# Layer 1's maxima over the whole array, from a copy of one head's queries that is zero outside the head, and a new order of the mixed phase

## The chip, the cores and the metric

The kernel runs on one core of a Trainium2 chip. The metric is device time in microseconds of one launch, which works through all sixteen graphs of the input; lower is better. "Before" is the kernel as it stands, "the change" the edited one.

## The reference, cut to what matters

Sixteen graphs of 512 nodes with 256 channels pass through two attention layers. Layer 0 has one head with a 0/1 mask, layer 1 eight heads of 32 channels with a weight per edge:

```python
# layer 0
scores = jnp.einsum('bod,bid->boi', q, k) / denom
scores = jnp.where(mask, -1e+18, scores)
attn = jax.nn.softmax(scores, axis=2)
ctx = jnp.einsum('boi,bie->boe', attn, node_fts) @ Wc
x = layer_norm(node_fts + ctx)
# layer 1: H = 8 heads, DK = 32
logits = jnp.einsum('bhqd,bhkd->bhqk', q, k) / np.sqrt(DK)
logits = logits + jnp.log(jnp.clip(adj, ADJ_MIN, None))[:, None, :, :]
attn = jax.nn.softmax(logits, axis=-1)
out = jnp.einsum('bhqk,bhkd->bhqd', attn, v)
out = out @ Wo.T + bo
x = layer_norm(x + out)
```

The softmax of layer 1 is computed as exp(logit - row maximum) times the clipped edge weight, divided by its sum. The row maxima are taken from a product of rounded queries and keys alone; they only shift the exponent.

## The kernel before

Every engine follows one list of stages, written out as a table. A phase of the mixed kind works on three graphs at once: the tail of graph t (project, stats1, norm1, output), the back of graph i (layer 1: scores1, masks, values1, denominators1, maxima of the second group of heads) and the front of graph j (layer 0, then q1, k1, v and the maxima of the first group). The list `SCHEDULE` sets the order of the mixed phase, `FIRST` that of the opening one and `LAST` that of the one that has no front any more. Each engine takes from the list, in that order, the stages that it has a part in, so one list fixes five queues. There are 15 mixed phases (one of them without a tail), between an opening phase for graph 0 and the closing ones.

The eight heads are two groups g of four heads h; 128 channels of a group lie on 128 partitions, head h on partitions 32h to 32h+31. The names that the rows show are:

- `max1` (g, n): TensorE (L709) multiplies 128 queries of one head by its 512 keys, with 32 rows of the array, into one of four shared `misc` banks of PSUM; VectorE (L1026) reduces the 512 columns to a negated maximum in `mx`. There are 32 a phase. n runs over query tile t and head h, with h fastest, so that neighbours in the list lie in different row groups of the array.
- `mrow1` (L714, L1032): the maxima of a group, turned into a row; after it the row goes by DMA into the stack `QS`.
- `scores1` (L730, ScalarE's exponential L868): keys x queries from the stacks `QS` and `KS` of 97 rows (three 32-row parts and the row of maxima), into two banks `scores`. `mask` (L1168 on GpSimd, L1011 on VectorE for the pairs that the list names) multiplies the result `PR` by the edge weights `CLIP`. A quad is four such products; `PR` has three buffers, quad modulo 3.
- `values1`, `denominators1` (L753): four 32-column products each, side by side in four column groups of the array, eight instructions a quad.
- `q0`, `q1`, `k1` (L609), `u` (L619), `v` (L631), `max0` (L661, L663), `scores0` (L674, L678, L679), `context0` (L687), `transpose` (L696), `project` (L775): products over the whole array. Their banks are drained by ScalarE or VectorE. Products of full 4-byte operands (L687, L696, L714, L753) are executed in two passes, and the profile counts both: four products of L753 in the program are eight in a row of it.
- `high_output` (L886, ScalarE) and `low_output` (L1083, VectorE) split the normalised output into `OTH` and `OTL`, which `project` multiplies.

The `misc` banks are handed out in the order of the list, modulo four; a fill waits until the use before it in the same bank is drained. TensorE takes its instructions in order, so that a product that waits holds everything behind it. The operand of a maximum is cut out like this:

```python
t, h = divmod(n, PER_GROUP)
part = slice(DK * h, DK * (h + 1))
pe.matmul(bank[:], Q1H[part, g, P * t:P * (t + 1)], K1H[part, g, :],
          start=True, stop=True).then_inc(misc_filled, 1)
```

## Time and profile before

| | us |
|---|---|
| median of the 3 runs | 1225.13 |
| the runs | 1222.51, 1225.13, 1558.84 |
| the profiled execution | 1222.59 |
| its span | 1220.8 |
| opening phase (0 to 78.58) | 78.58 |
| 15 mixed phases (78.58 to 1146.20) | 1067.62 |
| one of them (504.04 to 575.38) | 71.34 |
| closing phases (1146.20 to 1220.80) | 74.60 |

Shares of the span in which an engine is busy: TensorE (PE) 94%, its weight loads (PEld) 56%, VectorE (DVE) 77%, ScalarE (ACT) 43%, GpSimd (POOL) 60%. The 1.8 us between the profiled execution's time and its span lie around the span. A phase is counted from the first instruction of `mrow1` of group 0 (L714) to the next one; all times "at 5xx" are those of the phase that begins at 504.04. A duration of a product that the profile shows is from its start to its modelled end; products overlap in the pipeline, so what one costs TensorE is the distance from its start to the start of the next.

### The profile page before, as it was taken

How to read it: one execution, taken by the hardware profiler on the slowest of the kernel's cores; microseconds unless marked ns; L12 is line 12 of the kernel's file. 1: busy time of each engine (PE TensorE's matmuls, PEld its weight loads, DVE VectorE, ACT ScalarE, POOL GpSimd, SP SyncE). 2: the span in 40 equal slices, each digit the busy share in tenths (PEclk: the TensorE clock that was granted, in tenths of full speed). 3: DMA queues.
4: the chain of work that ended last, by engine and by line, in shares of the span. 5: the costliest groups of instructions: out<-in, count | busy, mean ns of one | idle time of the engine just before them, and what ended most of it. 6: DMA issues, size and time to landing. Idle time of an engine off the chain costs nothing.

```text
span 1220.8 us, 21304 instructions
## 1 busy us (share of the span) xinstructions
PE 1146.4 (94%) x6474; PEld 684.3 (56%) x6474; DVE 934.1 (77%) x1733; ACT 524.4 (43%) x1021; POOL 738.0 (60%) x353
## 2 busy tenths in 40 slices
PE   7789999999999999999999999999999999999883
PEld 6555564656556465564656556464655646565431
DVE  4465877969687796968779696877969688796874
ACT  3233444445344444534444453444445344444431
POOL 1026486584848658484865848487584848757462
PEclk9889999999999999999999999999999999999887
DMA  3051331405132140513314051331405133140310
GB/s 130 1 139 35 107 85 45 129 17 143 46 108 82 43 129 17 142 48 107 82 41 131 17 140 50 106 84 41 132 17 139 50 103 86 39 133 17 90 31 17
DMA packets 69652, 94.67 MB, mean 78 GB/s; under 512 B 14081, under 2 KB 32769, under 8 KB 69634
## 3 DMA queue, kind: packets, MB, share of 16 engines
q1 hardware_dynamic: 69634, 94.44, 27.5%
q8 instruction: 10, 0.16, 0.1%
q14 instruction: 8, 0.07, 0.0%
HBM read 35.40 MB, written 8.39 MB: 36 GB/s over the span
## 4 chain that ended last, share of the span: by engine, by line
PE 40%; DVE 23%; POOL 18%; issue 12%; ACT 5%; DVEq 0%; POOLq 0%; DMA 0%; ACTq 0%; SPq 0%
PE misc L609 11%; DVE mx L1026 8%; POOL PR L1168 8%; PE scores L730 6%; PE misc L631 4%; PE misc L619 3%; POOL z L1182 3%; POOL res L1151 3%; PE misc L661 2%; PE misc L709 2%; DVE PR L1011 2%; PE values L753 2%; PE values L775 2%; DVE K1L L990 2%; DVE sums_w L1073 2%
## 5 line engine op out<-in xcount | busy, mean ns | idle before, releaser
L1168 POOL TENSOR_TENSOR PR<-PR,CLIP 128x1024 f32<-128x1024 f32 x217 | 543.3, 2528 | 372.8 <-ACT PR L868 372.8
L1026 DVE TENSOR_REDUCE mx<-misc 128x1 f32<-128x512 f32 x512 | 322.4, 680 | 92.7 <-PE misc L709 92.4
L868 ACT ACTIVATE PR<-scores 128x512 f32<-128x512 f32 x512 | 279.2, 601 | 226.6 <-PE scores L730 217.8
L730 PE MATMUL scores<-QS,KS 97*128 97x512 f32 x512 | 196.4, 460 | 9.0 <-issue 3.5
L753 PE MATMUL values<-PR,V 128*32 128x512 f32 x1024 | 133.2, 603 | 14.5 <-DVE PR L1011 14.4
L753 PE MATMUL denominators<-PR,ones 128*32 128x512 f32 x1024 | 133.9, 605 | 0.8 <-DVE z L1092 0.3
L730 PEld LDWEIGHTS scores<-QS,KS 97*128 97x128 f32 x512 | 89.6, 193 | 68.3 <-ACT PR L868 36.3
L709 PE MATMUL misc<-K1H,Q1H 32*128 32x512 f32 x512 | 119.4, 500 | 6.7 <-DVE K1L L990 1.6
L687 PE MATMUL misc<-U,P 128*128 128x257 f32 x512 | 121.8, 386 | 0.0
L1073 DVE RECIPROCAL sums_w<-sums_w 128x128 f32<-128x128 f32 x128 | 114.0, 924 | 7.0 <-ACT sums_w L881 4.2
L709 PEld LDWEIGHTS misc<-K1H,Q1H 32*128 32x128 f32 x512 | 48.0, 183 | 119.2 <-DVE mx L1026 63.6
L687 PEld LDWEIGHTS misc<-U,P 128*128 128x128 f32 x512 | 94.4, 189 | 20.0 <-issue 3.8
L856 ACT ACTIVATE P<-misc 128x512 f32<-128x512 f32 x64 | 38.3, 598 | 96.4 <-PE misc L679 96.4
L753 PEld LDWEIGHTS values<-PR,V 128*32 128x32 f32 x1024 | 25.1, 109 | 68.9 <-issue 44.4
L1011 DVE TENSOR_TENSOR PR<-PR,CLIP 128x1024 f32<-128x1024 f32 x39 | 59.6, 1535 | 1.9 <-ACT PR L868 1.8
L674 PE MATMUL misc<-Q0H,XTH 128*128 128x512 f32 x128 | 58.9, 460 | 0.0
L834 ACT COPY V<-misc 128x512 f32<-128x512 f32 x32 | 18.8, 586 | 89.7 <-PE misc L631 89.7
L1182 POOL TENSOR_TENSOR z<-z,spread 128x1024 f32<-128x1024 f32 x16 | 38.2, 2390 | 28.8 <-DVE z L1108 28.8
L990 DVE SCALAR_TENSOR_TENSOR Q1L<-misc,cols,Q1H 128x512 fp32r<-128x512 f32 x32 | 24.0, 751 | 39.6 <-ACT Q1H L829 39.6
L753 PEld LDWEIGHTS denominators<-PR,ones 128*32 128x32 f32 x1024 | 22.4, 108 | 52.7 <-issue 46.2
L674 PE MATMUL misc<-Q0L,XTH 128*128 128x512 f32 x128 | 50.9, 398 | 0.0
L674 PE MATMUL misc<-Q0H,XTL 128*128 128x512 f32 x128 | 50.8, 397 | 0.0
(160 smaller groups left out, 1896.3 us busy)
## 6 DMA issues: line engine op xcount, KB each, us to landing
ADJ<-adj_t SPq DMA_DIRECT2D x16, 1024.0 KB, 6.0
QS<-Q1H SPq DMA_DIRECT2D x256, 64.0 KB, 2.0
KS<-K1H SPq DMA_DIRECT2D x256, 64.0 KB, 2.0
P<-x_t SPq DMA_DIRECT2D x16, 512.0 KB, 3.8
X<-x SPq DMA_DIRECT2D x16, 512.0 KB, 3.7
QS<-Q1L SPq DMA_DIRECT2D x128, 64.0 KB, 2.0
KS<-K1L SPq DMA_DIRECT2D x128, 64.0 KB, 2.0
out<-z SPq DMA_DIRECT2D x16, 512.0 KB, 2.9
```

Source lines behind the costliest of these rows:

```text
L609: mm = pe.matmul(bank[:], w[:, k, P * c:P * (c + 1)], s[:, k, :], start=(n == 0), stop=(n == len(terms) - 1))
L674: pe.matmul(bank[:], kk[:, c, rows_k], qq[:, c, :], start=(n == 0), stop=False)
L687: mm = pe.matmul(bank[:, 0:D + 1], P0[:, k, P * t:P * (t + 1)], U[:, k, 0:D + 1], start=(k == 0), stop=(k == T - 1))
L709: pe.matmul(bank[:], Q1H[part, g, P * t:P * (t + 1)], K1H[part, g, :], start=True, stop=True).then_inc(misc_filled, 1)
L730: pe.matmul(ST[n][:], KS[:, h, P * k:P * (k + 1)], QS[:, h, :], start=True, stop=True).then_inc(scores_filled, 1)
L753: mm = pe.matmul(bank[DK * h:DK * (h + 1), :], w, PR[quad % WEIGHT_BUFFERS][:, h, :], start=(k == 0), stop=(k == T - 1))
L868: act.activation(PR[quad % WEIGHT_BUFFERS][:, h, :], ST[n][:], ACT.Exp, scale=SCALE1).then_inc(exp_done, 1)
L1011: dve.tensor_tensor(w, w, clipped, ALU.mult).then_inc(masked_dve, 1)
L1026: dve.tensor_reduce(mx1[:, g, h, t:t + 1], misc_bank(ph, "max1", g, n)[:], AX.X, ALU.max, negate=True).then_inc(misc_drained["dve"], 1)
L1073: dve.reciprocal(sums_w[:, q], sums_w[:, q]).then_inc(back_step, 1)
L1168: pool.tensor_tensor(w, w, clipped, ALU.mult).then_inc(masked_pool, 1)
L1182: pool.tensor_tensor(z[:], z[:], all_rows(S_G1), ALU.mult).then_inc(pool_step1, 1)
```

## The change

The queries of one head are copied by ScalarE into `QZ[:, h, :]`, an array that was set to zero once, so that 96 of its 128 rows are zero. A maximum then is a product of all 128 rows, `QZ[:, h]` by `K1H[:, g]`. There are four such copies a group, eight a phase, as a new stage `alone` (g, h). n now runs over head and query tile with the tile fastest. The list of the mixed phase is written anew; `FIRST` and `LAST` get the copies put in and are otherwise the same. VectorE clears `QZ` once at the start.

```diff
 SCHEDULE = [
-    ("reciprocal", 1, 0), ("skip_back",), ("split", 0), ("split", 1), ("max1", 1, 0), ("reciprocal", 1, 1),
...
+    ("reciprocal", 1, 0), ("alone", 1, 0), ("split", 0), ("split", 1), ("alone", 1, 1), ("max1", 1, 0),
...
+        QZ = sb("QZ", [P, PER_GROUP, N], F32R)
...
+        def alone(ph, g, h):
+
+            return HEADS * (ph.i if g else ph.j) + PER_GROUP * g + h + 1
...
                 bank = fill(ph, "max1", g, n)
-                t, h = divmod(n, PER_GROUP)
-                part = slice(DK * h, DK * (h + 1))
-                pe.matmul(bank[:], Q1H[part, g, P * t:P * (t + 1)], K1H[part, g, :],
+                h, t = divmod(n, T)
+                if t == 0:
+                    pe.wait_ge(head_alone, alone(ph, g, h))
+                pe.matmul(bank[:], QZ[:, h, P * t:P * (t + 1)], K1H[:, g, :],
                           start=True, stop=True).then_inc(misc_filled, 1)
...
+            def put_alone(ph, g, h):
+                part = slice(DK * h, DK * (h + 1))
+                if g == 0:
+                    act.wait_ge(hi_written, ph.j * (C * len(SPLIT)) + nth_split(ph, "q1", 0))
+                    if ph.back:
+                        wait_filled(act, ph, "max1", 1, T * h + T - 1)
+                else:
+                    act.wait_ge(misc_drained["dve"], misc.count_before(ph, "max1", 0, T * h + T - 1))
+                act.copy(QZ[part, h, :], Q1H[part, g, :]).then_inc(head_alone, 1)
...
+            dve.memset(QZ[:].bitcast(F32), 0.0).then_inc(consts_set, 1)
...
             def max1(ph, g, n):
-                t, h = divmod(n, PER_GROUP)
+                h, t = divmod(n, T)
```

The new list moves work on every engine. TensorE at the end of a mixed phase, from `k1` of channel half 1 to `mrow1` (maxima are L709 before and L722 after, the products of 32 columns L753 and L766, `v` L631 and L643). Before:

```order
L609 MATMUL misc<-XNL,Wk_high 128x512 x2
L709 MATMUL misc<-K1H,Q1H 128x512
L753 MATMUL denominators<-PR,ones 32x512 x4
L709 MATMUL misc<-K1H,Q1H 128x512 x2
L753 MATMUL values<-PR,V 32x512 x4
L709 MATMUL misc<-K1H,Q1H 128x512 x3
L631 MATMUL misc<-Wv_high,XNH 128x256 x2
...
L709 MATMUL misc<-K1H,Q1H 128x512 x2
L631 MATMUL misc<-Wv_high,XNH 128x256 x2
...
L714 MATMUL misc<-ident,mx 16x128
```

and with the change:

```order
L621 MATMUL misc<-XNL,Wk_high 128x512 x2
L722 MATMUL misc<-K1H,QZ 128x512 x3
L766 MATMUL denominators<-PR,ones 32x512 x4
L766 MATMUL values<-PR,V 32x512 x8
L722 MATMUL misc<-K1H,QZ 128x512 x4
L643 MATMUL misc<-Wv_high,XNH 128x256 x2
...
L722 MATMUL misc<-K1H,QZ 128x512 x5
L643 MATMUL misc<-Wv_high,XNH 128x256 x2
...
L727 MATMUL misc<-ident,mx 16x128
```

Twelve maxima instead of eight now stand behind `k1`, and the products of 32 columns, which stood between maxima in two places, have become one group.

VectorE in the same stretch, from the low part of `q1` to the end of the phase (`K1L`, `Q1L` are L990 and L1015, the maxima L1026 and L1051, the clipping L999 and L1024, `OTL` L1083 and L1108). Before:

```order
L990 SCALAR_TENSOR_TENSOR Q1L<-misc,cols,Q1H 128x512
L990 SCALAR_TENSOR_TENSOR K1L<-misc,cols,K1H 128x512
L1079 TENSOR_TENSOR sums_v<-sums_v,sums_w 128x512
L1026 TENSOR_REDUCE mx<-misc 128x1 x3
L990 SCALAR_TENSOR_TENSOR Q1L<-misc,cols,Q1H 128x512
L1026 TENSOR_REDUCE mx<-misc 128x1 x3
L999 TENSOR_SCALAR CLIP<-ADJ 128x2048
L1026 TENSOR_REDUCE mx<-misc 128x1 x2
L990 SCALAR_TENSOR_TENSOR K1L<-misc,cols,K1H 128x512
L1026 TENSOR_REDUCE mx<-misc 128x1 x8
L1083 TENSOR_TENSOR OTL<-sums_v,OTH 128x512
L1032 CAST nm_0<-misc 16x128
```

and with the change:

```order
L1015 SCALAR_TENSOR_TENSOR Q1L<-misc,cols,Q1H 128x512
L1015 SCALAR_TENSOR_TENSOR K1L<-misc,cols,K1H 128x512
L1015 SCALAR_TENSOR_TENSOR Q1L<-misc,cols,Q1H 128x512
L1104 TENSOR_TENSOR sums_v<-sums_v,sums_w 128x512
L1051 TENSOR_REDUCE mx<-misc 128x1 x4
L1024 TENSOR_SCALAR CLIP<-ADJ 128x2048
L1015 SCALAR_TENSOR_TENSOR K1L<-misc,cols,K1H 128x512
L1051 TENSOR_REDUCE mx<-misc 128x1 x3
L1108 TENSOR_TENSOR OTL<-sums_v,OTH 128x512
L1051 TENSOR_REDUCE mx<-misc 128x1 x9
L1057 CAST nm_0<-misc 16x128
```

All sixteen maxima of the group now come after the second `Q1L`; three stood ahead of it.

ScalarE in the loop, where `OTH` (L886 and L909) is written for the projection (L868 and L891 are exponentials, L840 and L863 drain `u`; ISA and REGISTER_ALU rows are waits and their counters). Before:

```order
L840 COPY U<-misc 128x258
L885 ISA
L886 CAST OTH<-sums_v 128x512
L867 REGISTER_ALU
L868 ACTIVATE PR<-scores 128x512
```

and with the change:

```order
L863 COPY U<-misc 128x258
L890 REGISTER_ALU
L891 ACTIVATE PR<-scores 128x512
L890 REGISTER_ALU
L891 ACTIVATE PR<-scores 128x512
L908 ISA
L909 CAST OTH<-sums_v 128x512
```

Two exponentials have moved ahead of `OTH`.

## Rows read from the trace of the kernel before

**Rows 1.** Windows: span, busy us (xcount) of PE, PEld, DVE, ACT, POOL, granted clock, DMA.

```profile
504.04:575.38 71.34, 69.38 (x401) 41.39 (x401) 56.86 (x107) 32.29 (x63) 46.96 (x22) 1.00 0.28 81
78.58:1146.20 1067.62, 1038.89 (x5976) 618.19 (x5977) 843.04 (x1569) 483.24 (x943) 697.23 (x326) 1.00 0.28 79
1146.20:1220.80 74.60, 45.58 (x229) 20.42 (x228) 49.63 (x76) 22.25 (x41) 35.30 (x17) 0.74 0.14 38
```

**Rows 2.** Timeline, TensorE, maxima and their neighbours: start us, us, engine line op.

```profile
517.59 0.40 PE L663 MATMUL misc<-masked_bf,ABSENT 128*128 128x128 bf16 x4
517.91 0.50 PE L709 MATMUL misc<-K1H,Q1H 32*128 32x512 f32 x2
518.34 0.72 PE L730 MATMUL scores<-QS,KS 97*128 97x512 f32 x2
...
521.85 0.51 PE L709 MATMUL misc<-K1H,Q1H 32*128 32x512 f32 x4
522.28 1.92 PE L753 MATMUL values<-PR,V 128*32 128x512 f32 x16
524.14 0.50 PE L709 MATMUL misc<-K1H,Q1H 32*128 32x512 f32 x2
524.57 1.06 PE L753 MATMUL denominators<-PR,ones 128*32 128x512 f32 x8
525.57 0.50 PE L674 MATMUL misc<-Q0H,XTH 128*128 128x512 f32 x1
525.91 0.39 PE L674 MATMUL misc<-Q0H,XTL 128*128 128x512 f32 x1
526.14 0.39 PE L674 MATMUL misc<-Q0L,XTH 128*128 128x512 f32 x1
```

**Rows 3.** Timeline, TensorE, the start of the phase.

```profile
504.04 0.39 PE L714 MATMUL misc<-ident,mx 128*16 128x128 f32 x2
504.58 0.69 PE L709 MATMUL misc<-K1H,Q1H 32*128 32x512 f32 x2
505.79 1.01 PE L609 MATMUL misc<-XTH,A_high 128*128 128x512 f32 x2 [0.52 <-ACT XTH L822]
```

**Rows 4.** Timeline, TensorE, transposes and the wait for a mask.

```profile
550.61 1.08 PE L696 MATMUL misc<-ident,xn 128*128 128x128 f32 x4
551.45 0.77 PE L730 MATMUL scores<-QS,KS 97*128 97x512 f32 x2
...
555.26 1.06 PE L753 MATMUL values<-PR,V 128*32 128x512 f32 x8 [0.95 <-DVE PR L1011]
```

**Rows 5.** Timeline, TensorE, three maxima near the end, then v.

```profile
570.77 0.84 PE L709 MATMUL misc<-K1H,Q1H 32*128 32x512 f32 x3
571.71 0.50 PE L631 MATMUL misc<-Wv_high,XNH 128*128 128x256 f32 x2
```

**Rows 6.** Timeline, ScalarE, VectorE and TensorE around the projection.

```profile
516.37 0.62 ACT L886 CAST OTH<-sums_v 128x512 fp32r<-128x512 f32 x1
...
517.41 1.60 DVE L1083 TENSOR_TENSOR OTL<-sums_v,OTH 128x512 fp32r<-128x512 f32 x1
...
519.38 0.40 PE L775 MATMUL values<-Wo_high,OTL 128*128 128x256 f32 x2
```

**Rows 7.** Timeline, VectorE, clipping, low part of k1, six maxima.

```profile
566.79 1.22 DVE L999 TENSOR_SCALAR CLIP<-ADJ 128x2048 f32<-128x2048 f32 x1
...
569.12 0.74 DVE L990 SCALAR_TENSOR_TENSOR K1L<-misc,cols,K1H 128x512 fp32r<-128x512 f32 x1
569.78 3.67 DVE L1026 TENSOR_REDUCE mx<-misc 128x1 f32<-128x512 f32 x6
```

**Rows 8.** Timeline, ScalarE, two copies from SBUF to SBUF.

```profile
576.45 1.15 ACT L822 CAST XTH<-P 128x512 fp32r<-128x512 f32 x2
```

**Rows 9.** Groups by line, VectorE, a memset of the start.

```profile
L919 DVE MEMSET PR<- 128x256 f32 x1 | 0.3, 272 | 0.0
```

**Rows 10.** The page, costliest groups: the masks on GpSimd.

```profile
L1168 POOL TENSOR_TENSOR PR<-PR,CLIP 128x1024 f32<-128x1024 f32 x217 | 543.3, 2528 | 372.8 <-ACT PR L868 372.8
```

More of the change, by code:

```diff
@@ L150, in is_back @@
 def is_back(stage):
-    return stage[0] in BACK or stage[:2] in (("max1", 1), ("mrow1", 1))
+    return stage[0] in BACK or stage[:2] in (("alone", 1), ("max1", 1), ("mrow1", 1))
 def is_tail(stage):
@@ L365, in two_layer_graph_attention @@
         hi_written = sem("hi_written")
+        head_alone = sem("head_alone")
         bias_built = sem("bias_built")
@@ L404, in two_layer_graph_attention @@
         FOLDED_LOADS, FIRST_LOADS, REST_LOADS = 2, 1 + 1, 4 + 1
-        CONSTS = 9
+        CONSTS = 10
         block = ctx.enter_context(nc.Block())
@@ L421, in graph_of, with nth_split @@
             return ph.t if g == GROUPS - 1 else ph.i
+        def alone(ph, g, h):
+            return HEADS * (ph.i if g else ph.j) + PER_GROUP * g + h + 1
+        def nth_split(ph, *stage):
+            return [s for s in ORDERS[ph.kind] if s[0] in SPLIT].index(stage) + 1
         def mask_operands(quad, pair):
@@ L899, in _ @@
                 "k1": lambda ph, c: hi(ph, "k1", c, K1H, BK1),
+                "alone": put_alone,
                 "v": lambda ph, n: rows_out(ph, "v", n, V),
```

9 lines of the change are left out of this document (5 added, 4 removed), and 73 rows, old and new, of tables (FIRST, LAST, SCHEDULE).

## The prediction

> **What bounds the kernel now.** I read the windows first. The 15 mixed phases take 1067.62 of the span's 1220.8 us, 71.2 each, and the one that I follow takes 71.34, with TensorE busy for 69.38 of it at the full clock, VectorE for 56.86, GpSimd for 46.96 and ScalarE for 32.29 [rows 1]. So TensorE's queue sets the phase; what matters is what an instruction costs there and where the queue stands still. The timeline of TensorE tells both, by distances from start to start.
>
> The price of a whole-array product of 512 columns is 0.23 us (525.91 to 526.14) [rows 2]. Maxima go otherwise: two of them hold TensorE for 0.43 us (517.91 to 518.34) and four for the same 0.43 (521.85 to 522.28) [rows 2]. Row groups work side by side, but a run costs 0.43 whether it holds one or four. On top, each change between the whole array and a divided one costs some 0.10: the first product after a divided stretch takes 0.34 and the next 0.23 [rows 2]; on the way in, four short products take 0.32 up to a maximum (517.59 to 517.91) [rows 2], where my price for them, 0.21, makes 0.11.
>
> The queue stands still in few places. At the phase's start, mrow1 and two maxima take 1.75 us (504.04 to 505.79), and q0 then waits for XTH from ScalarE [rows 3]; 0.43 for the maxima and 0.32 for mrow1 leave 1.0 lost. Transposes waiting for xn take 0.84 instead of 0.44 (550.61 to 551.45), a sum waits 0.95 for a mask of VectorE [rows 4], and three maxima near the end take 0.94 instead of 0.43, since their banks are still to be drained [rows 5]. With some 1.0 in small pieces, mostly around score products, I count 3.9 us of waiting and 67.4 of work a phase.
>
> **The price of the maxima.** The new list has the same 32 a phase. Before they stand in 13 runs: 13 x 0.43 = 5.6 us. After, 32 x 0.23 = 7.4. That is +1.8. The clock is at its upper level of 2.4 GHz (granted 1.00) in this stretch and TensorE's activity rises if anything, so I leave the price at that level.
>
> A rule of the Trainium skill speaks against the change: "TensorE: Matmul & The Clock Gate", section "Why this matters for your kernels", has small-K products in distinct row groups run concurrently, 3.07 times faster for four, and a single K=32 product as long as a K=128 one. The trace here gives 4 x 0.23 / 0.43 = 2.1 for a run of four and worse than that page for a single one. By the page a run would cost 4 x 0.23 / 3.07 = 0.30, the runs before 3.9 us in all, and the change +3.5 where the rows give +1.8: 25 us more over 15 phases. The rows are of this kernel and decide.
>
> **The changes of mode.** Going through the list of before, TensorE's divided stretches (maxima and the 32-column sums, where they adjoin each other) number 12, so 24 changes. After, maxima no longer divide the array and the sums stand in 6 groups, 12 changes. 12 x 0.10 = -1.2. The sums' own price stays: sixteen in a row cost 1.86 (522.28 to 524.14), eight cost 1.00 (524.57 to 525.57) [rows 2], so each switch of bank costs about 0.14, and both lists have 14 stretches of one bank.
>
> Work on the array therefore changes by 1.8 - 1.2 = **+0.6 us a phase** before any wait is looked at. The new order has to win it back from the 3.9 us of waiting.
>
> **The waits.** I follow the new list with the prices above, in the time of the phase shown, and ask where it stands against before.
> - Start. One maximum instead of two stands ahead of q0, so that is cheaper, but q0 waits for XTH either way. On ScalarE a copy of a head stands ahead of XTH where a copy of the sums stood before; a copy from SBUF to SBUF costs 0.58 (1.15 for two) [rows 8]. No gain until q0. ABSENT is now built ahead of both low parts of q0, and max0 needs the second one: 0.1 lost.
> - Projection. Before, OTH is written at 516.37, OTL by VectorE from 517.41 for 1.60 us, and TensorE asks for OTL at 519.38 [rows 6], 0.4 after it is there. Now two exponentials precede OTH, which puts it at about 517.7, and a max1 and a max0 precede OTL, which then ends near 519.9. TensorE asks for it near 519.3. It waits 0.6, and everything behind it: three maxima, a score pair, scores0. GpSimd gets the last mask of quad 2 about 1 us later, and with it the norm of the tail.
> - Middle, up to context0. Eleven maxima cost 2.5 instead of four runs of 0.43, and two groups of sums stand alone: +0.9. I have TensorE 1.7 us behind by context0.
> - Transposes. GpSimd has lost one mask (3,0 goes to VectorE) and reaches the norm of the front a little earlier, while TensorE comes later: the 0.4 and the 0.95 of [rows 4] go. What is late next is ScalarE: scores1 of quad 6 wait for exponentials, 0.7 again in front of the sums. 1.1 behind at q1.
> - End. q1, k1, q1 and two score pairs stand together: 3 x 1.4 + 2 x 0.5 us, so that the second Q1H is ready near 563.1. From then on VectorE has Q1L, normalise, sixteen maxima, clip, K1L and OTL without a gap: maxima at 0.61 (3.67 for six), clip 1.15, K1L 0.66, the starts being 566.79, 569.12 and 569.78 [rows 7]; I take 0.68 for the other three. 16 x 0.61 + 1.15 + 4 x 0.68 = 13.6, end at 576.7, and mrow1 follows there instead of at 575.38: +1.4. Before, three of the maxima were done ahead of the second Q1L. v must wait for their banks in turn, so TensorE has nothing to overtake with.
> - Next start. The sums are copied before v now, and the start's loss of 1.0 shrinks by 0.3 since TensorE arrives later than ScalarE's work allows.
>
> So the walk gives +1.1 a phase, the bare price of the work with waits as before +0.6. I take +0.9: 15 x 0.9 = **+13.5**. The eight copies are 8 x 0.58 = 4.6 us on ScalarE, busy 32.29 of 71.34; they hide there behind waits for TensorE, except the one ahead of XTH. If that cover is gone they cost 0.58 each where an exponential waits for one: 15 x 0.58 = 9 for each such place.
>
> **Opening and closing.** The memset of QZ is 128x2048; 128x256 takes 0.272 [rows 9], so at most eight times that, 2.2, and nothing at the least if it lies beside the first loads. I take 0.5. In the opening, four copies stand ahead of K1H and VectorE sets the pace of maxima: +0.5. The closing phase of 74.60 has the clock at 0.74 on average, so partly at 1.2 GHz [rows 1]; its sixteen maxima stand in 8 runs: 8 x 0.43 = 3.4 becomes 16 x 0.23 = 3.7, and up to 16 changes of mode at 0.10 go. That is -1.3, or -2.6 if all of it ran at half the clock, but the chain there goes through exponentials and masks as well, and three copies stand among those (1.7 if each is on the path). I take -0.5, bounds -3 and +2.
>
> **Sum.** 13.5 + 0.5 + 0.5 - 0.5 = +14. The profiled execution's 1222.6 (span 1220.8 plus 1.8 around it) becomes 1236.6; the median of the runs stands 2.5 above it, so **1239 us**, +1.1%.
>
> **Rivals.**
> 1. The new order takes out half of the waiting (for it: it does remove the waits of [rows 4], and a single whole-array product can be put anywhere without a change of mode; against: I found new waits at OTL and at the end). 3.9 falls to 1.9, a phase changes by 0.6 - 2.0 = -1.4, 15 phases by -21: 1225 - 21 = 1204.
> 2. Slower, through GpSimd. It runs the chain norm of the tail, two steps of z, two of res, three masks, norm of the front, and then xn for the transposes. A mask costs 2.5 [rows 10] and the other steps about as much; seven of them are 17.5 us. With the last mask of quad 2 late by 1.1 and norm1 behind four maxima, z begins near 530.5 and xn is there near 549.8, while TensorE asks at 551.5. The slack is 1.7. If z begins later than 532.2, the chain decides and every further microsecond is added to the phase; 1.5 beyond it, with the rest of my walk, makes +2.4 a phase, +36: 1261.
> 3. The change costs what the work costs and the waits cancel: +0.6 x 15 = +9, 1234. A whole-array maximum that took 0.27, as one behind a short product may, would add 32 x 0.04 = 1.3 a phase: +19 on top of the forecast, 1257.
> 4. The maxima do not bound anything, because VectorE's reduce (0.61 against 0.23) paces them anyway: then only the order counts, and the time stays within 5 us of 1225.
>
> **Chances.** Forecast and the first half of rival 3 together 0.50 (1228 to 1248); rival 1 0.20, of which 0.08 beyond 2%; rival 2 and the dear product 0.18; rival 4 0.12. The range that leaves out 1 in 10 on either side is 1204 to 1260; the unknown costs of opening and closing (-3 to +4) lie within it. Two per cent, 24.5 us, is about what a measurement can tell from no change: faster 0.09, same 0.68, slower 0.23.
>
> **What would show it.** In the profile after: the distance between whole-array maxima in a run, 0.23 each; mixed phases of about 72.2 us between the mrow1 of group 0; no wait of a sum for VectorE's mask near 555; a wait of the projection for OTL of about 0.6; VectorE without a gap from the second Q1L to the end of the phase. The prediction is wrong if a phase is under 70.5 (waits gone that I kept) or over 73.5 (GpSimd's chain, or a price of 0.27), or if the clock in the closing phase moves by more than the copies cost.

## The result and the profile after

The change takes 1247.15 us (median of 1236.40, 1244.99, 1249.32 and 1251.35) against 1229.33 for the kernel before in the same comparison. The ratio of its runs to those of before is 1.0158, with a 95% interval of 1.0111 to 1.0205: slower by some 1.6%, 8 us above the 1239 of the prediction and inside its range. The 1229.33 counts a slow run of before, of 1558.84 us, which the ratio leaves out; its other three runs have a median of 1225.13. The profiled execution took 1236.4 us, the shortest of the four, with a span of 1234.6; that is 0.2 us from the forecast for it, 1236.6. That agreement is luck, as the parts show.

Windows of the kernel with the change: the phase that begins at 507.62, the 15 mixed phases, the closing (columns as in [rows 1]):

```profile
507.62:579.07 71.45, 69.97 (x399) 45.03 (x401) 57.36 (x106) 37.09 (x72) 47.86 (x22) 1.00 0.29 80
76.82:1154.26 1077.44, 1048.18 (x5947) 672.42 (x5977) 861.01 (x1569) 555.94 (x1065) 709.64 (x326) 1.00 0.28 79
1154.26:1234.60 80.34, 48.66 (x228) 23.23 (x228) 48.83 (x75) 24.37 (x44) 34.29 (x17) 0.74 0.13 36
```

Against [rows 1] the mixed phases are 9.8 us longer, the closing 5.7, the opening 1.8 shorter: together the 13.8 by which the spans differ. The mean of 0.65 a phase hides two kinds. Cut at the mrow1 of group 0, ten mixed phases take 71.4 to 71.7 us, nearly as before (71.3 to 71.4), four take 73.35, and the very first, without a tail, takes 69.5 instead of 68.75. The phase of the first row is a short one, only 0.1 above its counterpart.

What bounds it is told by the page's chain that ended last. Before, the chain went through GpSimd for 18% and VectorE for 23%; now:

```profile
PE 77%; DVE 12%; issue 4%; ACT 4%; POOL 0%; DVEq 0%; ACTq 0%; DMA 0%; POOLq 0%; SPq 0%
```

So TensorE's queue is the bound in the main, with VectorE for an eighth of the time. The timeline of TensorE answers [rows 2] (price of a product), [rows 3] (start) and [rows 4] (transposes, then sums):

```profile
507.62 0.39 PE L727 MATMUL misc<-ident,mx 128*16 128x128 f32 x2 [0.19 <-DVE mx L1051]
508.75 0.49 PE L722 MATMUL misc<-K1H,QZ 128*128 128x512 f32 x1 [0.74 <-ACT QZ L853]
509.26 1.02 PE L621 MATMUL misc<-XTH,A_high 128*128 128x512 f32 x2
...
525.52 0.85 PE L722 MATMUL misc<-K1H,QZ 128*128 128x512 f32 x3
526.21 0.63 PE L743 MATMUL scores<-QS,KS 97*128 97x512 f32 x2
...
532.75 0.50 PE L722 MATMUL misc<-K1H,QZ 128*128 128x512 f32 x1
533.09 0.39 PE L686 MATMUL misc<-Q0H,XTH 128*128 128x512 f32 x1
...
555.20 0.60 PE L708 MATMUL misc<-ident,xn 128*128 128x128 f32 x4
555.84 0.99 PE L743 MATMUL scores<-QS,KS 97*128 97x512 f32 x2
556.76 1.07 PE L766 MATMUL denominators<-PR,ones 128*32 128x512 f32 x8
```

Three maxima take 0.69 (525.52 to 526.21), 0.23 each; one behind a divided stretch takes 0.34 (532.75 to 533.09), the 0.10 of a change of mode again. That is the price where the banks are free. Where VectorE still drains them it is higher, as in the last two runs of the phase:

```profile
572.59 1.20 PE L722 MATMUL misc<-K1H,QZ 128*128 128x512 f32 x4
573.88 0.51 PE L643 MATMUL misc<-Wv_high,XNH 128*128 128x256 f32 x2
...
575.42 1.68 PE L722 MATMUL misc<-K1H,QZ 128*128 128x512 f32 x5
577.20 0.51 PE L643 MATMUL misc<-Wv_high,XNH 128*128 128x256 f32 x2
```

Four take 1.29 and five 1.78. From mrow1 to q0 it is 1.64 instead of 1.75, and the wait is for the first copy now, 0.74, where it was 0.52 for XTH. Transposes and sums no longer wait for xn or for a mask.

The waits of TensorE over all mixed phases say the same in four rows, "us in total, times, longest":

```profile
PE misc L722 <- ACT QZ L853: 11.3, 15, 0.8
PE values L788 <- DVE OTL L1108: 6.6, 4, 1.7
PE misc L727 <- DVE mx L1051: 2.5, 14, 0.2
PE misc L727 <- issue: 2.4, 15, 0.2
```

Before these were 14.4 for VectorE's mask and 7.1 for XTH. The OTL row has four waits: they are the four long phases.

A short and a long phase at the projection ([rows 6] before). VectorE and TensorE in the phase from 507.62:

```profile
521.51 0.69 DVE L1040 TENSOR_REDUCE bounds<-misc 128x1 f32<-128x512 f32 x1
522.12 0.68 DVE L1108 TENSOR_TENSOR OTL<-sums_v,OTH 128x512 fp32r<-128x512 f32 x1
...
523.14 0.40 PE L788 MATMUL values<-Wo_high,OTL 128*128 128x256 f32 x2
```

and in the phase from 721.9:

```profile
735.80 0.69 DVE L1040 TENSOR_REDUCE bounds<-misc 128x1 f32<-128x512 f32 x1
736.41 2.89 DVE L1108 TENSOR_TENSOR OTL<-sums_v,OTH 128x512 fp32r<-128x512 f32 x1
...
739.36 0.39 PE L788 MATMUL values<-Wo_high,OTL 128*128 128x256 f32 x1 [1.66 <-DVE OTL L1108]
```

One and the same subtraction takes 0.68 or 2.89 us. In the raw records GpSimd's next mask starts at 522.14 in the first, 0.02 behind OTL, and at 736.40 in the second, 0.01 ahead of it. So it goes in all mixed phases with a tail: OTL took 0.68 wherever it started 0.02 us or more ahead of the mask, and 2.89 to 2.91 in the four where it started with it or 0.01 behind. Below 0.01 us the recorded starts don't tell who was first: in the second profile of this kernel (change_again) an OTL took 0.68 with the mask recorded 0.005 ahead of it, and another 2.92 with the mask recorded 0.004 behind.

### The profile page after: what moved, and what is told of

It is laid out like the page before. It is cut to its first block, busy times and chain, and to the rows that moved or that the text cites. A ratio compares the mean times of both kernels' runs of the same rounds, so it can differ in the third digit from the quotient of the medians.

```text
span 1234.6 us, 21671 instructions
## 1 busy us (share of the span) xinstructions
PE 1156.3 (94%) x6443; PEld 741.2 (60%) x6474; DVE 950.9 (77%) x1734; ACT 601.7 (49%) x1149; POOL 749.4 (61%) x353
## 4 chain that ended last, share of the span: by engine, by line
PE 77%; DVE 12%; issue 4%; ACT 4%; POOL 0%; DVEq 0%; ACTq 0%; DMA 0%; POOLq 0%; SPq 0%
PE scores L743 11%; PE misc L621 10%; PE misc L699 9%; PE denominators L766 7%; PE misc L686 7%; PE misc L722 7%; DVE mx L1051 6%; PE values L766 6%; PE misc L643 4%; PE misc L631 3%; PE misc L673 3%; PE values L788 2%; PE denominators L788 2%; DVE OTL L1108 2%; PE misc L708 1%
## 5 line engine op out<-in xcount | busy, mean ns | idle before, releaser
L891 ACT ACTIVATE PR<-scores 128x512 f32<-128x512 f32 x512 | 280.3, 606 | 225.4 <-PE scores L743 122.6
L1051 DVE TENSOR_REDUCE mx<-misc 128x1 f32<-128x512 f32 x512 | 323.5, 681 | 27.5 <-PE misc L722 26.9
L722 PE MATMUL misc<-K1H,QZ 128*128 128x512 f32 x512 | 183.9, 441 | 20.6 <-ACT QZ L853 14.5
L722 PEld LDWEIGHTS misc<-K1H,QZ 128*128 128x128 f32 x512 | 93.6, 192 | 92.0 <-DVE mx L1051 35.1
L766 PE MATMUL denominators<-PR,ones 128*32 128x512 f32 x1024 | 138.3, 602 | 0.6 <-DVE z L1117 0.3
L743 PEld LDWEIGHTS scores<-QS,KS 97*128 97x128 f32 x512 | 95.4, 193 | 67.6 <-ACT PR L891 46.4
L766 PE MATMUL values<-PR,V 128*32 128x512 f32 x1024 | 129.3, 599 | 0.1
L1036 DVE TENSOR_TENSOR PR<-PR,CLIP 128x1024 f32<-128x1024 f32 x39 | 83.6, 2146 | 2.6 <-ACT PR L891 2.5
L853 ACT CAST QZ<-Q1H 32x512 fp32r<-32x512 f32 x128 | 78.7, 615 | 2.7
L766 PEld LDWEIGHTS values<-PR,V 128*32 128x32 f32 x1024 | 29.7, 109 | 68.8 <-issue 59.0
L1067 DVE TENSOR_SCALAR den<-misc 128x1 f32<-128x1 f32 x64 | 10.1, 158 | 72.5 <-PE misc L699 72.5
L766 PEld LDWEIGHTS denominators<-PR,ones 128*32 128x32 f32 x1024 | 28.7, 109 | 55.4 <-issue 44.7
L1207 POOL TENSOR_TENSOR z<-z,spread 128x1024 f32<-128x1024 f32 x16 | 38.2, 2385 | 33.8 <-DVE z L1133 33.8
L686 PE MATMUL misc<-Q0H,XTH 128*128 128x512 f32 x128 | 53.8, 420 | 0.0
L1209 POOL TENSOR_TENSOR z<-z,spread 128x1024 f32<-128x1024 f32 x16 | 50.4, 3150 | 1.3
```

The lines of the kernel that those rows point to most:

```text
L686: pe.matmul(bank[:], kk[:, c, rows_k], qq[:, c, :], start=(n == 0), stop=False)
L722: pe.matmul(bank[:], QZ[:, h, P * t:P * (t + 1)], K1H[:, g, :], start=True, stop=True).then_inc(misc_filled, 1)
L743: pe.matmul(ST[n][:], KS[:, h, P * k:P * (k + 1)], QS[:, h, :], start=True, stop=True).then_inc(scores_filled, 1)
L766: mm = pe.matmul(bank[DK * h:DK * (h + 1), :], w, PR[quad % WEIGHT_BUFFERS][:, h, :], start=(k == 0), stop=(k == T - 1))
L853: act.copy(QZ[part, h, :], Q1H[part, g, :]).then_inc(head_alone, 1)
L891: act.activation(PR[quad % WEIGHT_BUFFERS][:, h, :], ST[n][:], ACT.Exp, scale=SCALE1).then_inc(exp_done, 1)
```

## The experiments

Lengths of phases are distances between the starts of the first product of mrow1 of group 0; "mixed" is the usual length of one, and in brackets another that occurs. Medians and ratios are against the kernel before in the same comparison.

| kernel | opening | mixed | closing | median | ratio, 95% |
|---|---|---|---|---|---|
| before | 78.6 | 71.35 | 74.6 | | |
| the change | 76.8 | 71.4 (four 73.35) | 80.3 | 1247.15 | 1.0158, 1.0111 to 1.0205 |
| change_again | 81.2 | 71.4 (nine 73.4) | 80.6 | 1249.52 | 1.0203, 1.0173 to 1.0233 |
| order_only | 78.5 | 73.92 | 75.1 | 1259.67 | 1.0294, 1.0257 to 1.0331 |
| array_no_copies | 74.9 | 72.49 | 73.8 | 1235.73 | 1.0098, 1.0063 to 1.0132 |
| array_old_order | 81.5 | 75.95 (six 77.5) | 83.1 | 1309.32 | 1.0688, 1.0648 to 1.0728 |
| array_old_early | 78.8 | 73.22 (three 74.8) | 75.3 | 1256.80 | 1.0278, 1.0259 to 1.0296 |
| change_no_copies | 75.3 | 73.3 | 73.3 | 1246.98 | 1.0202, 1.0185 to 1.0220 |
| oth_early | 79.4 | 71.4 (four 73.4) | 80.1 | 1240.04 | 1.0161, 1.0103 to 1.0219 |
| otl_early | 79.0 | 72.55 | 79.7 | 1245.90 | 1.0194, 1.0177 to 1.0210 |
| otl_early_last | 78.7 | 72.55 | 73.4 | 1240.13 | 1.0147, 1.0124 to 1.0169 |
| small_mask | 81.1 | 71.4 | 80.0 | 1230.23 | 1.0058, 1.0036 to 1.0081 |
| otl_early_bank | 79.0 | 71.67 | 75.7 | 1228.96 | 1.0030, 1.0006 to 1.0054 |
| hybrid | 76.3 | 71.35 | 74.8 | 1223.91 | 1.0007, 0.9983 to 1.0031 |

Where not said otherwise, a diff is against the change.

### The two halves apart

**order_only**: the new list without its copies, the row-group products of before.

```diff
-                h, t = divmod(n, T)
-                pe.matmul(bank[:], QZ[:, h, P * t:P * (t + 1)], K1H[:, g, :],
+                t, h = divmod(n, PER_GROUP)
+                pe.matmul(bank[:], Q1H[part, g, P * t:P * (t + 1)], K1H[part, g, :],
```

> The new list of the mixed phase with the maxima as before: 32 rows, heads side by side, no QZ and no copies. Theory 1 (prices of the array): in the new list the maxima stand in 16 runs of up to four, 16 x 0.43 = 6.9 us instead of 5.6, and divided stretches number 15 instead of 12, six changes more at 0.10. That is +1.9 us of work a phase against the kernel before; with the 3.4 us of waiting that the changed kernel shows outside its long phases (71.4 less 68.0 of work), mixed phases of 72.7 us or more and +20 to +30 us in all: the new list only pays with whole-array products. Theory 2 (VectorE's reduce paces the maxima, whatever a product costs): the mixed phases stay at the changed kernel's 71.4, +0 to +5 us against before. Both expect closing and opening phases as before, since nothing is copied there.

**array_no_copies**: the kernel before with whole-array products that read all queries instead of one head's (diff against before).

```diff
-                pe.matmul(bank[:], Q1H[part, g, P * t:P * (t + 1)], K1H[part, g, :],
+                pe.matmul(bank[:], Q1H[:, g, P * t:P * (t + 1)], K1H[:, g, :],
```

> The old list, and the maxima over 128 rows taken straight from Q1H, so that they sum over all four heads of a group (the output is not the reference's): the price of the whole array alone, with no copy on ScalarE. Theory 1: 32 x 0.23 = 7.4 instead of 13 x 0.43 = 5.6, and 22 changes of mode instead of 24: +1.6 us of work a phase, of which the wait at three maxima near the end may take up 0.5: mixed phases of 72.3 to 72.9, +15 to +24 us in all. Theory 2: phases within 0.2 of 71.34. A gain would say that a change of mode costs more than 0.10.

**array_old_order**: the list of before with the copies put in, each near the maxima that need it, and the products of the change (diff of one line of the list, against before).

```diff
-    ("max1", 0, 1), ("max1", 0, 2), ("scores1", 7, 1), ("q1", 1), ("high_output", 0), ("max1", 0, 3),
...
+    ("scores1", 7, 1), ("q1", 1), ("alone", 0, 1), ("high_output", 0), ("max1", 0, 3), ("max1", 0, 4),
```

> The change's products and copies with the old list, the copies put in some stages ahead of the first product that needs each: against the run without copies it tells what eight copies a phase cost. Theory 1 (copies lie beside waits of ScalarE): mixed phases within 0.3 of the run without copies, and the closing phase some 5 us longer than before, as in the changed kernel, since LAST is the changed kernel's. Theory 3 (ScalarE's copies are what the change costs): each copy of 0.6 us ahead of an exponential or of XTH adds to the phase, +1 to +3 us a phase on top.

The runs of order_only are 35 us above before, more than the 20 to 30 expected; those of array_no_copies 11 us, less than the 15 to 24, with the mixed phase as expected; and the copies of array_old_order cost 3.5 us a phase, more than either theory had.

The whole-array product alone costs 1.14 us a phase in the old list. The landmarks show where: context0 begins 1.3 later against the phase's start, q1 1.2, v 1.4. The new list with the products of before costs 2.57. TensorE's waits of order_only (100 to 1150 us):

```profile
PE values L784 <- DVE OTL L1103: 10.8, 14, 0.8
PE misc L640 <- DVE mx L1046: 9.8, 14, 0.7
```

The first is a wait for OTL, as the prediction expected of the change (0.6), but from another cause: OTL takes 2.6 us here, since GpSimd's mask starts 0.3 ahead of it. The second is v, whose banks VectorE still holds. Both halves are losses, 1.1 and 2.6 us a phase, and together they lose nothing in a short phase. They don't add: in the new list the whole-array product is worth 0.6 (73.92 to 73.30 in change_no_copies, below), in the old one it costs 1.1. The change is slow neither by its product nor by its order as such.

The copies are the third part, and in the wrong place they cost more than the rest. TensorE's waits of array_old_order in the same stretch, and then the timeline at a phase's start:

```profile
PE misc L722 <- ACT QZ L853: 51.2, 40, 1.5
```

```profile
537.38 0.73 PE L722 MATMUL misc<-K1H,QZ 128*128 128x512 f32 x2 [1.48 <-ACT QZ L853]
537.95 1.10 PE L621 MATMUL misc<-XTH,A_high 128*128 128x512 f32 x2
538.85 1.05 PE L621 MATMUL misc<-XTH,A_low 128*128 128x512 f32 x2
```

40 waits make 51.2 us, 3.7 for each of some 14 phases. Behind this wait of 1.48 the clock falls; the last section comes back to it.

**array_old_early**: array_old_order with each copy moved ahead in the list, and all four first in the closing (diff of one line, against array_old_order).

```diff
-    ("scores1", 7, 1), ("q1", 1), ("alone", 0, 1), ("high_output", 0), ("max1", 0, 3), ("max1", 0, 4),
+    ("scores1", 7, 1), ("alone", 0, 2), ("q1", 1), ("alone", 0, 3), ("high_output", 0), ("max1", 0, 3),
```

> The old list with whole-array products and copies again, the copies put some stages earlier than in the first such run, where TensorE waited for them 3.9 us a phase. Theory 1 (the copies cost by their place, not by their work): mixed phases of 72.5 to 74 instead of 76 to 77.5, near the 72.5 of the old list without copies. Theory 3 (eight copies of 0.62 us load ScalarE as such): phases stay at 75 or more.

It takes 73.22, 0.7 above array_no_copies and 2.7 below array_old_order: of the 3.5 us that late copies add, 2.7 were their place. The wait that stays is the one at the start of the phase, 1.3 at most.

**change_no_copies**: the new list without copies, whole-array products that read all queries.

```diff
-                if t == 0:
-                    pe.wait_ge(head_alone, alone(ph, g, h))
-                pe.matmul(bank[:], QZ[:, h, P * t:P * (t + 1)], K1H[:, g, :],
+                pe.matmul(bank[:], Q1H[:, g, P * t:P * (t + 1)], K1H[:, g, :],
```

> The changed kernel with no copies and no wait for them: the products take all 128 rows of Q1H, so that they sum over four heads (the output is not the reference's). It tells what the copies cost in the new list. Theory 1 (array work is what the mixed phase costs, the copies cost the closing phase and the start of each phase, where one stands ahead of XTH): closing phase back to 73.5 to 75 from 80.3, mixed phases 0.3 to 0.7 shorter than 71.4, in all 10 to 16 us under the changed kernel. Theory 3 (copies hidden everywhere): closing and mixed phases as in the changed kernel. Whether the long phases of 73.4 stay depends on where OTL falls against GpSimd's masks, which this kernel shifts too; no side is forecast there.

Removing work made the mixed phases longer: all but the first two take 73.3, and TensorE waits for OTL in those 13:

```profile
PE values L783 <- DVE OTL L1103: 21.6, 13, 1.7
```

The 0.3 to 0.7 us a phase that were expected to be saved don't show in the sum, since GpSimd's mask is now at least level with OTL every time. Like compared with like, a long phase is 0.07 shorter without copies (73.30 against 73.37). TensorE begins q0 0.6 earlier in it (1.01 us from the phase's start instead of 1.65), but the first score pair only 0.05 earlier (5.02, 5.07). Two phases gain more: the first one takes 68.3 instead of 69.5 and the second, the only short one with a tail, 71.1 instead of 71.7. So the copies cost next to nothing in a long phase; what they cost in a short one isn't settled by a single phase. The closing is another matter: 73.3 without them, 80.3 with them.

### OTL

**oth_early**: ScalarE writes OTH ahead of two exponentials.

```diff
-    ("scores1", 2, 0), ("high_output", 1), ("max1", 1, 2), ("max0", 2), ("low_output", 1), ("max1", 1, 3),
+    ("high_output", 1), ("scores1", 2, 0), ("max1", 1, 2), ("max0", 2), ("low_output", 1), ("max1", 1, 3),
```

> The changed kernel with one stage moved in its list: OTH is written before the two exponentials of scores1 (2,0), not behind them. Theory 1 (the projection waits for OTL, and OTL takes 2.9 us instead of 0.7 where GpSimd's mask starts 0.03 us earlier than it): OTL starts 1 us earlier, the projection does not wait, phases of 70.8 to 71.2 and none of 73.4; 5 to 12 us under the changed kernel, closing and opening as there. Rival: OTL then meets another mask of GpSimd and takes 2 to 3 us in every phase, phases stay over 71.4.

Nothing changes, four long phases included, and the 5 to 12 us that were expected don't come. OTH isn't what OTL waits for: on VectorE it stands behind the reduce of max0(2), as the two timelines above show.

**otl_early**: OTL also moves ahead of that reduce.

```diff
-    ("scores1", 2, 0), ("high_output", 1), ("max1", 1, 2), ("max0", 2), ("low_output", 1), ("max1", 1, 3),
+    ("high_output", 1), ("scores1", 2, 0), ("max1", 1, 2), ("low_output", 1), ("max0", 2), ("max1", 1, 3),
```

> The changed kernel with two stages moved: OTH ahead of the exponentials of scores1 (2,0), and OTL ahead of VectorE's reduce of max0 (2) (the run before moved OTH alone, and OTL stayed behind that reduce, so nothing changed). Theory 1 (OTL and a mask of GpSimd exclude each other; it is late only when it is asked for just after a mask has begun): OTL is asked for while a mask runs, gets its turn when that ends, near 14.6 us after mrow1 as in the short phases, and every phase has 71.4 us, none 73.4; 4 to 10 us under the changed kernel in the mean of runs. Rival: OTL loses to the next mask as well (2.9 us each time), phases of 73 or more throughout.

The two kinds of phases are gone, and all behind the first take 72.5 to 72.6, not the 71.4 expected. OTL begins 2.1 us behind the start of the mask that runs, takes 1.30, and no wait for it is left. But the reduce behind it drains its bank later, and the waits of TensorE have a new row:

```profile
PE misc L722 <- DVE bounds L1040: 13.1, 14, 1.0
```

That is most of the 1.1 us above the short phase.

**otl_early_last**: this, and in the closing list the four copies first.

```diff
-    ("alone", 1, 0), ("max1", 1, 0), ("reciprocal", 1, 0), ("reciprocal", 1, 1), ("reciprocal", 1, 2),
+    ("alone", 1, 0), ("alone", 1, 1), ("alone", 1, 2), ("alone", 1, 3), ("max1", 1, 0), ("reciprocal", 1, 0),
```

> As the run with OTH and OTL early, and in the closing phase all four copies at its start, where ScalarE had been idle for 2 us, instead of each ahead of the products that need it. Theory 1 (the closing phase lost 5 us to copies between exponentials): the closing phase shrinks from 80.3 to 75 to 77, and the whole is 8 to 14 us under the changed kernel, about as fast as the kernel before (-2 to +6 us). Rival (the closing phase is longer for other reasons, as its clock): it stays at 79 to 81.

The closing falls from 79.7 to 73.4, further than the 75 to 77 expected, and the median by 5.8. The whole stays 18 us above before, where 6 at most were expected: the mixed phases of 72.55 are still there. The waits of TensorE in the closing, first of the change (in otl_early these two rows are 3.1 and 1.5):

```profile
PE misc L722 <- ACT QZ L853: 3.2, 3, 1.8
PE misc L722 <- DVE mx L1051: 1.5, 1, 1.5
```

then of otl_early_last, where the row of mx is gone:

```profile
PE misc L722 <- ACT QZ L853: 0.8, 1, 0.8
```

ScalarE in the closing of the change shows why:

```profile
1161.74 0.62 ACT L909 CAST OTH<-sums_v 128x512 fp32r<-128x512 f32 x1 [1.86 <-DVE sums_v L1104]
1162.38 0.62 ACT L853 CAST QZ<-Q1H 32x512 fp32r<-32x512 f32 x1
1163.03 1.08 ACT L891 ACTIVATE PR<-scores 128x512 f32<-128x512 f32 x2
```

The second copy could be made at once (otl_early_last makes all four 0.5 us after its closing begins), but it stands in the list behind OTH, and OTH waits 1.86 for VectorE. Against otl_early, which differs by this edit alone, the two rows explain 3.8 of the 6.3 us. For the rest the windows show TensorE busy for 45.30 instead of 48.15 us on the same 228 instructions, at the same mean granted clock of 0.76. The records of the clock have 18.3 us of that busy time at the lower level, instead of 22.8 in otl_early. Those 4.5 us at half the clock are some 2.2 us of time, so that 6.0 of the 6.3 are accounted for. That the shorter waits kept the clock up isn't shown: oth_early waits longer for copies in its closing than the change (4.3 us) and has less busy time at the lower level (21.2 against 24.3).

**small_mask**: the change with GpSimd's colliding mask cut short. It leaves out the edge weights of one pair of heads in all but four columns, so its output is not the reference's.

```diff
+                if ph.kind == "steady" and (quad, pair) == (1, 1):
+                    w, clipped = w[:, :, 0:4], clipped[:, :, 0:4]
```

> The changed kernel with one of GpSimd's masks in each phase cut to 4 columns: the one that starts within 0.03 us of OTL's addition on VectorE (POOL at 522.14, 2.9 us long). What is left out is the mask of all but four columns of one pair of heads; the output is no longer the reference's. Theory: OTL's addition is held for the whole of that mask when the mask starts first (2.9 us instead of 0.7), and this and nothing else makes a phase long. Then OTL takes 0.6 to 0.8 us in every phase, every phase between the first and the last is 71.4 us or a little less, none is 73.4, and a run ends 8 us below the profiled run of the change (4 long phases x 1.93), near 1228. Rival: the two kinds of phases come from something else (the clock, a transfer, another pair of operations); then OTL's 2.9 us goes but phases of 73.4 stay, or OTL goes on taking 2.9 us.

Each part of the theory held: OTL takes 0.68 to 0.76 in every mixed phase, although it starts within 0.06 us of the mask as before (0.12 in one); no phase takes 73.4; the median is 1230.23, and eight runs lie within 3.7 us. The group of OTL over the whole kernel, here

```profile
L1108 DVE TENSOR_TENSOR OTL<-sums_v,OTH 128x512 fp32r<-128x512 f32 x32 | 23.4, 732 | 1.4 <-ACT OTH L909 1.4
```

has a mean of 732 ns; the change has 999 over the whole kernel. The rival is out. The narrow spread proves less: the kernel before spread over 14 us in the 29 runs of this comparison.

**change_again**: the change, unedited, once more.

> The changed kernel, unedited, for the spread of its times. Theory: each phase is long or short by a coin that falls within 0.03 us, and each long one adds 1.93 us, so that twelve runs spread over 1229 (no long phase) to 1258 (fifteen), most of them 1234 to 1252, and a profile shows phases of 71.4 and of 73.4 in another number and in other places than the four of before. The kernel with the mask cut to 4 columns, which has no long phase, spread over 3.7 us in 8 runs, the one with OTL issued early over 5.3 us in 12. Rival: the spread comes from something that the other kernels have too; then this one's is 4 to 6 us wide as well and the long phases sit in the same places.

Six runs took 1245.76 to 1254.46 us. The profiled one has nine long phases, in other places, and a span of 1248.9: 14.3 above the first profile, of which the mixed phases are 9.7 (five more long ones, 5 x 1.93 = 9.7) and the opening 4.4. In eight of the nine OTL met the mask. In the ninth it was the addition in front of it, with the same price:

```profile
233.24 0.69 DVE L1040 TENSOR_REDUCE bounds<-misc 128x1 f32<-128x512 f32 x1 [0.27 <-PE misc L675]
233.85 2.97 DVE L1104 TENSOR_TENSOR sums_v<-sums_v,sums_w 128x512 f32<-128x512 f32 x1
236.74 0.68 DVE L1051 TENSOR_REDUCE mx<-misc 128x1 f32<-128x512 f32 x1
```

The mask of that moment starts at 233.86, which to the hundredth is the same time. So the kernel's time is not one number: the ten runs of the change in two comparisons spread over 18 us, its two profiles had four and nine long phases. That long phases make the spread of the runs that weren't profiled is inferred, since a time alone doesn't show its phases. The six runs of change_again alone spread over 8.7 us, and those of the kernel before beside them over 7.6, so here the spread decides nothing; what shows the two kinds of phases is the two profiles.

### Repairs

**otl_early_bank**: otl_early_last with the fifth maximum moved behind the projection, since it waited for the bank.

```diff
-    ("skip_back",), ("max0", 3), ("floor",), ("max1", 1, 4), ("shift0",), ("project",), ("max1", 1, 5),
+    ("skip_back",), ("max0", 3), ("floor",), ("shift0",), ("project",), ("max1", 1, 4), ("max1", 1, 5),
```

> The changed kernel with three edits of its lists. OTH and OTL are issued ahead of the exponential and the reduce that they stood behind, the closing list makes the four copies first, and the fifth piece of the maxima is moved behind the project step, since with OTL early (72.55 us a phase) TensorE waited 0.96 us for a bank of maxima that VectorE had not yet bounded. Theory: that wait was what the earlier OTL gave back; with the piece moved it goes, every phase takes 71.4 us whatever GpSimd does, the closing takes 73.4, and the whole is 1224 to 1230, within 0.5% of the kernel before. Rival: the wait only moves to the next piece behind the project step or to the stats, since VectorE itself is the one that is late there; then phases stay at 72.5 and the whole at 1238 to 1242.

Every phase behind the first takes 71.6 to 71.8, so nearly all of the 1.1 is back (0.3 short of the 71.4 expected), and the runs lie within 5.3 us. The closing took 75.7 instead of 73.4, on the same list and with nearly the same waits as in otl_early_last, at a granted clock of 0.72 instead of 0.76, with 24.5 us of TensorE's busy time at the lower level instead of 18.3. The median, 1228.96, and the ratio, 1.003, are as expected: the change is mended to within 0.3% of the kernel before, and gains nothing.

**hybrid**: list and products of before in the mixed phases, those of the change in the opening and the closing.

```diff
+                if ph.kind == "steady":
+                    t, h = divmod(n, PER_GROUP)
+                    part = slice(DK * h, DK * (h + 1))
+                    pe.matmul(bank[:], Q1H[part, g, P * t:P * (t + 1)], K1H[part, g, :],
+                              start=True, stop=True).then_inc(misc_filled, 1)
+                    return
```

> The list and the row-group products of the kernel before in the fifteen mixed phases, and the whole-array products with their copies only in the opening and the closing phase, with the copies first in the closing. Theory, by sums of stretches of other runs: the opening takes 75 to 79 us (78.6 before), the mixed phases 71.35 each as before, the closing 73.4 instead of 74.6; the whole is 1220 to 1226, between 4 us below the kernel before and 1 above: no difference that matters. Rival: the mixed phase cannot take the row-group products beside the closing's without the copies of ScalarE falling into its last stretch, and the phases next to the ends pay 1 to 2 us each; then 1226 to 1230.

The mixed phases take 71.35 as before. The closing takes 74.8 instead of the 73.4 expected. Its waits add to about the same as in otl_early_last (14.7 and 14.5 us), but 20.6 us of TensorE's busy time are at the lower level instead of 18.3, although the mean granted clock is higher (0.78 against 0.76): the mean doesn't tell how much work runs slowly. The opening takes 76.3, and the ratio is 1.0007 (0.9983 to 1.0031): no difference. No version that I ran is faster than the kernel before.

## Why the prediction was right, and where not

The sign was right, and the time too, by errors that nearly cancelled in the profiled run: the mixed phases came out 3.7 us under the forecast (9.8 against 13.5), the opening 2.8 under it (-1.8 against 1.0), the closing 6.2 over it (5.7 against -0.5). The second profile of the same kernel, 1250.7, is 14.1 us from the same forecast. So the agreement is luck, though the extra work on the array and the wait at OTL were there.

- **Price of a whole-array maximum**: right, 0.23, where its bank is free. The dear product of rival 3 (0.27) didn't come in such a run. But from the start of each run of maxima to the next other product the 32 take 9.8 us in the phase from 507.62, not the 7.4 of the sum (before, without the wait for XTH, 6.4 and not 5.6); the changes of mode are part of that, and most of the rest is in runs that VectorE's drains pace (five in 1.78).
- **Changes of mode**, 0.10 each: right where it can be read (0.34 against 0.23 at 532.75). The balance of work in the old list measures +1.14 (array_no_copies); but that list keeps the sums in 11 groups, against 6 in the new one, so only one of 12 divided stretches goes there and the same prices give 1.8 - 0.2 = +1.6. In the new list the work can't be read apart from the waits.
- **Start**: right. No gain until q0 (1.64 against 1.75); the wait for XTH turned into a longer one for the copy.
- **Projection**: the mechanism was right, OTL's place on VectorE decides, and the size wasn't a size. I took 1.60 us for OTL from [rows 6] and got a wait of 0.6 in each phase. It is 0 or 1.7, by whether VectorE or GpSimd starts first, within 0.03 us: 4 x 1.65 = 6.6 us here, 0.44 a phase, and twice that with nine long phases. The cause that I gave, OTH behind two exponentials, was wrong: oth_early changes nothing. order_only has a wait of 0.8 in every phase, near my 0.6, but from an OTL that takes 2.6 us there and not from OTH.
- **Middle and transposes**: context0 begins 1.1 behind in a short phase, and 1.7 less my 0.6 for OTL is 1.1: right. The waits of [rows 4] went, as predicted. But q1 is then 0.4 us ahead of before (51.86 against 52.22 from the phase's start), not 1.1 behind; the wait of 0.7 for exponentials in front of the sums isn't there. This is the step that failed in the mixed phase.
- **End**: VectorE's chain from the second Q1L was put at 13.6 and takes 13.84 (57.48 to 71.32 from the phase's start), with one gap of 0.23. Only it starts 1.6 us earlier than I had it, by the step before, so it costs 0.1 to 0.2 instead of 1.4. VectorE in that stretch ([rows 7] before):

```profile
565.09 0.75 DVE L1015 SCALAR_TENSOR_TENSOR Q1L<-misc,cols,Q1H 128x512 fp32r<-128x512 f32 x1 [0.61 <-ACT Q1H L842]
...
573.13 2.48 DVE L1051 TENSOR_REDUCE mx<-misc 128x1 f32<-128x512 f32 x4
575.85 3.08 DVE L1051 TENSOR_REDUCE mx<-misc 128x1 f32<-128x512 f32 x5 [0.23 <-PE misc L722]
```

- **A phase**: +0.9 predicted, +0.65 in this profile and +1.3 in the second one, 0.1 in a short phase, 2.0 in a long one. No phase is near the 72.2 that I gave as a sign.
- **Copies**: hidden in the mixed phase, except at its start: right for the long phases (0.07 by change_no_copies, and even the wait at the start is made up by the first score pair), open for the short ones. array_old_order and array_old_early show that it is so by their place only.
- **Opening**, +0.5 and +0.5: not settled. It took 76.8 and 81.2 in two profiles of the same kernel, at granted clocks of 0.91 and 0.89, and 74.9 to 81.5 in all kernels, so a memset of 2 us at most can't be seen.
- **Closing**, -0.5 with bounds of -3 and +2: wrong, it is +5.7 and outside of the bounds. I bounded the three copies by their length on ScalarE (1.7). What counts is what they stand behind: a copy waits for OTH, OTH for VectorE, and TensorE waits for all of it. otl_early_last takes 6.3 us back by moving three stages. Two prices failed here: the place in ScalarE's list, and the work at the lower clock. TensorE's waits in the closing add to 18.2 us instead of the 15.3 of before, and its busy time at the lower level is 24.3 instead of 20.2 us, some 2 us of time. Why more work fell to that level is open.
- **Rivals**: rival 1 is out, as waits came in place of those that went: the rows of TensorE's waits over the mixed phases add to 21.8 us before and to 22.8 after. Rival 2 is out: GpSimd has 0% of the chain that ended last, and none of TensorE's waits in the mixed phases. It does set the time by another way, through VectorE, which I hadn't listed: its mask in [rows 10] holds OTL. Rival 3's first half (+0.6 a phase, waits cancelling) is nearer to the mean of this profile (+0.65) than the forecast. Rival 4 is out as a whole, but half of it is true: a phase with OTL short costs what it did before, and VectorE does pace the runs at the phase's end.

## What to carry to other kernels

A copy that depends on little should be issued where its source is ready, ahead of anything on its engine that waits; its price is that of the wait that it stands behind, not its length. Where a phase shows two lengths, look for two engines whose operations start together, and move one of them well clear (here OTL, 2.1 us behind the start of one mask and 0.7 ahead of the next) rather than hope for the better order; then look at what drains later for it. Two halves of a change that each lose alone (1.1 and 2.6 us a phase here) can come out even together, so a list is judged with the products that it was made for.

## What the runs showed of the hardware

**VectorE's operations with two operands in SBUF and GpSimd's masks exclude each other.** OTL takes 0.68 us when it starts first; the mask then takes 2.91 instead of 2.4. When the mask starts first, OTL takes as long as the mask has left, and 0.5 to 0.6 more: 2.9 if it began with the mask, 2.61 at 0.3 us into it (order_only), 1.60 at 1.8 (before), 1.30 at 2.1 (otl_early). The profile counts the time that it is held as busy. VectorE's reduces out of PSUM keep their 0.6 to 0.7 beside a running mask. The Trainium skill, "SBUF — State Buffer", section "SBUF: two separate sides", states that of an operation with two SBUF inputs on VectorE and one of GpSimd the first gets a shared pair of ports for its whole length and the other blocks; the numbers here agree, and add that a lead of 0.02 us decides it. The masks that VectorE does itself pay too. Their group on the page had a mean of 1535 ns before; after:

```profile
L1036 DVE TENSOR_TENSOR PR<-PR,CLIP 128x1024 f32<-128x1024 f32 x39 | 83.6, 2146 | 2.6 <-ACT PR L891 2.5
L1209 POOL TENSOR_TENSOR z<-z,spread 128x1024 f32<-128x1024 f32 x16 | 50.4, 3150 | 1.3
```

and so does a step of z on GpSimd (2381 before). In the phase from 507.62 a mask of VectorE starts 0.40 us into one step of z and takes 3.07, where one that meets nothing took 1.23 before (at 544.25); the next step of z starts while that mask runs and takes 3.27. The 24 us more on VectorE's masks don't reach TensorE, which has no wait for PR left in the mixed phases.

**The clock can fall behind a wait inside the busy phase, and need not.** Windows of array_old_order, ahead of the wait of 1.48 us and behind it (the third number from the end is the granted clock):

```profile
533.50:537.90 4.40, 2.92 (x20) 2.19 (x19) 3.34 (x7) 3.34 (x7) 0.00 (x0) 1.00 0.53 133
538.85:541.41 2.56, 2.56 (x8) 1.99 (x6) 2.32 (x4) 0.62 (x1) 0.00 (x0) 0.50 0.44 106
```

The granted clock is 1.00 and then 0.50, the lower of its levels, 1.2 instead of 2.4 GHz. Six products of q0 take these 2.56 us, 0.43 each instead of 0.23, and full speed is back at 542.16. The same wait of 1.48 stands at the start of all 14 mixed phases behind the first. Behind six of them the clock fell, and these are the six phases of 77.5 us; behind the other eight it stayed, as in the phase before this one:

```profile
461.44:465.00 3.56, 3.54 (x14) 2.56 (x15) 3.07 (x6) 1.67 (x3) 0.00 (x0) 1.00 0.39 94
```

The difference in length, 1.5 us, is what a fall costs. In array_old_early the clock fell in three mixed phases, the three of 74.8 us. In the change it stayed at 1.00 behind the wait of 0.74 at the same place and behind the 1.66 for OTL at 739.36. So the length of a wait alone doesn't decide it; what does, these runs don't show.
